# A graph kernel in which SyncE fetches one chunk of 128 edge rows in 64 with one-row DMAs, in place of GpSimd's indirect gather

## The reference

```python
def _gcn_conv(x, src, dst, W, b, n):
    deg = segment_sum(ones_like(dst), dst, n)
    dinv = rsqrt(maximum(deg, 1.0))
    out = segment_sum((x @ W)[src] * (dinv[src] * dinv[dst])[:, None], dst, n)
    return out + b

def _gat_conv(x, src, dst, W, a_src, a_dst, b, n):
    h = (x @ W).reshape(n, H, HID)                    # H = 4, HID = 64
    e = (einsum(h, a_src))[src] + (einsum(h, a_dst))[dst]
    e = where(e > 0, e, 0.2 * e)
    w = exp(e - segment_max(e, dst, n)[dst])
    att = w / segment_sum(w, dst, n)[dst]
    return segment_sum(att[:, :, None] * h[src], dst, n).reshape(n, H * HID) + b

h = batch_norm(relu(_gcn_conv(layernorm(x), ...)))
h = elu(batch_norm(_gat_conv(h, ...)))
h = elu(batch_norm(_gat_conv(h, ...)))
x = x + h
x = x + experts(layernorm(x))                         # 8 experts, top 2
```

## Time and profile before

| | us |
|---|---|
| median of 3 runs | 8761.01 (8760.34 to 8766.04) |
| the profiled execution | 8765.76 |
| its span in the trace | 8763.9 |
| GCN edge stage (391 to 2476 in the span) | 2085 |
| GAT edge stages (2646 to 4735, 5113 to 7202) | 2089 each |
| POOL busy | 5700.4, 65% |
| DVE busy | 4991.6, 57% |
| PE busy | 4960.7, 57% |
| ACT busy | 1673.4, 19% |

### The profile page before, as it was taken

The page is one execution under the profiler, slowest core; times in us unless marked ns, Lnnn a source line. Parts: engine busy times, 40 slices in busy tenths (PEclk is TensorE's granted clock), DMA queues, the critical chain, the costliest instruction groups (busy, mean ns, idle before and its releaser), DMA issues. The chain is left out here.

```text
span 8763.9 us, 120133 instructions
## 1 busy us (share of the span) xinstructions
PE 4960.7 (57%) x24975; PEld 3898.8 (44%) x24976; DVE 4991.6 (57%) x11850; ACT 1673.4 (19%) x7117; POOL 5700.4 (65%) x5675
## 2 busy tenths in 40 slices
PE   3433333333354666666665656666666663369994
PEld 2333333333333444444444434444444442349994
DVE  7722222222237777777777777777777777953335
ACT  3400000000031111111111421111111112253331
POOL 0177777777747777777777467777777776605552
PEclk9999999999997777777777877777777786559997
DMA  5411111111124555555553135555555540212226
GB/s 191 147 26 26 26 26 26 26 26 26 26 68 108 133 133 132 133 133 133 132 133 95 35 99 132 132 133 133 133 133 132 133 127 28 76 63 70 70 70 208
DMA packets 488664, 834.96 MB, mean 95 GB/s; under 512 B 119275, under 2 KB 332904, under 8 KB 481958
## 3 DMA queue, kind: packets, MB, share of 16 engines
q0 software_dynamic: 232576, 551.37, 24.7%
q1 hardware_dynamic: 242740, 270.23, 10.4%
q10 hardware_dynamic: 13298, 12.80, 0.4%
HBM read 751.87 MB, written 82.11 MB: 95 GB/s over the span
## 5 line engine op out<-in xcount | busy, mean ns | idle before, releaser
L707 POOL DMA_INDIRECT gat_rows<-gat_table,gat_idx x3328 | 3202.9, 962 | 1040.1 <-issue 902.4
L771 PE MATMUL gat_ps_sum<-gat_msg,gat_hot 128*128 128x260 f32 x6656 | 2395.4, 522 | 1113.4 <-DVE feat L790 1109.1
L771 PEld LDWEIGHTS gat_ps_sum<-gat_msg,gat_hot 128*128 128x128 f32 x6656 | 1641.9, 259 | 1487.5 <-DVE gat_msg L824 1132.6
L707 POOL DMA_INDIRECT gcn_rows<-gcn_table,gcn_idx x1664 | 1570.3, 944 | 857.8 <-issue 506.2
L771 PE MATMUL gcn_ps_sum<-gcn_rows,gcn_hot 128*128 128x64 f32 x3328 | 809.2, 425 | 1294.4 <-issue 946.6
L771 PEld LDWEIGHTS gcn_ps_sum<-gcn_rows,gcn_hot 128*128 128x128 f32 x3328 | 740.6, 327 | 1363.1 <-issue 1363.1
L790 DVE SCALAR_TENSOR_TENSOR feat<-gcn_ps_sum,in_first,feat 128x64 f32 x416 | 118.1, 284 | 1637.5 <-PE gcn_ps_sum L771 1637.5
L814 DVE TENSOR_TENSOR gat_logit<-gat_rows,gat_near 128x16 f32<-128x16 f32 x832 | 148.8, 179 | 1134.9 <-DMA gat_rows<-gat_table,gat_idx 1129.7
L756 PEld LDWEIGHTS gat_ps_near<-gat_tab,gat_hot_t 128*128 128x128 bf16 x6656 | 265.1, 102 | 898.9 <-issue 724.5
L756 PE MATMUL gat_ps_near<-gat_tab,gat_hot_t 128*128 128x24 bf16 x6656 | 312.1, 178 | 538.5 <-DVE gat_hot L802 534.7
L802 DVE TENSOR_TENSOR gat_hot<-gat_count,mod_t 128x512 f32<-128x512 f32 x832 | 566.5, 681 | 0.1
(11 more groups left out here) (331 smaller groups left out, 7358.4 us busy)
## 6 DMA issues: line engine op xcount, KB each, us to landing
gat_mod<-mod_rows SPq DMA_DIRECT2D x832, 128.0 KB
gi_mods<-mod_rows SPq DMA_DIRECT2D x52, 1024.0 KB, 4.6
gat_rows<-gat_table,gat_idx POOLq DMA_INDIRECT x3328
gcn_rows<-gcn_table,gcn_idx POOLq DMA_INDIRECT x1664, 2.4
gat_table<-feat SPq DMA_DIRECT2D x14, 1820.0 KB, 7.1
mix_rows<-y_rows SPq DMA_DIRECT2D x98, 256.0 KB, 5.1
xn_rows<-ffi_z SPq DMA_DIRECT2D x7, 1792.0 KB, 6.7
out_dram<-feat ACTq DMA_DIRECT2D x48, 256.0 KB
```

The costliest lines, as they stand in the source:

```text
L707: pool.indirect_dma_start(B["rows"][:, c, k, :], None, table, bass.IndirectOffsetOnAxis(ap=B["idx"][:, c, k:k + 1], axis=0)).then_inc(rows ...
L771: mm = pe.matmul(B["ps_sum"][b][:, 0:width], B["hot"][:, j, k, :], rhs, start=(k == 0), stop=(k == CH - 1))
```

## The change

In every edge stage, of each 16 groups the one with number 7 (AT) gets only three indirect DMAs from POOL. The rows of its fourth chunk come another way, all of it issued by SP (`send`, which takes the place of `send_mods` and now runs in the GCN stage too):

1. `bring`, 32 groups ahead: a DMA loads the chunk's 128 source numbers to `ahead_idx`, one partition.
2. `fetch`, 16 groups ahead: in each of 16 turns SP loads eight of the numbers to registers and issues eight DMAs of one row each, from the table to one partition of `ahead` (two buffers).
3. `push`, in turn 6 of the 16: SP waits until all 128 rows are there and until group 16n+3 has been used, and copies `ahead` to the slot of group 16n+7 with one DMA (semaphore `pushed`).
4. `free`, once in 16 turns: waits for the copy before last and for the source numbers.

ACT, PE (GCN) and DVE (GAT) wait for `pushed` in addition where they deal with that group. The loop bodies hold 16 turns instead of 4, SP's 32. The counts by which engines wait for rows are worked out by `landed`, since one slot in four gets 16 increments fewer in each 16 groups.

```diff
+AHEAD, AT = 16, 7
+BURST = P // AHEAD
@@ def edge_buffers
+    B.update(ahead=T.sb("ahead", [P, 2, width]), ahead_idx=T.sb("ahead_idx", [1, 2, P], I32))
@@ def fast_edges
     def gather(pool):
         def group(i, c):
-            g = RING * i + c
+            j, g = c % RING, AHEAD * i + c
             pool.wait_ge(idx_staged, g + 1)
             wait(pool, rows_used, g - 3)
             pool.sem_inc(begun, 1)
-            for k in range(CH):
-                pool.indirect_dma_start(B["rows"][:, c, k, :], None, table,
...
+            for k in range(CH - (c == AT)):
+                pool.indirect_dma_start(B["rows"][:, j, k, :], None, table,
...
-        pace(pool, NG, [(group, 0)], RING)
-
-    def send_mods(sp):
-        def group(i, c):
-            g = RING * i + c
-            wait(sp, hot_built, g - 3)
-            sp.dma_start(B["mod"][:, c, :], mod_rows[one(g), :].to_broadcast([P, GE])).then_inc(mod_in[c], 16)
-        pace(sp, NG, [(group, 0)], RING)
+        pace(pool, NG, [(group, 0)], AHEAD)
+
+    def send(sp):
+        regs = [sp.alloc_register(f"{L}sp_row{r}") for r in range(BURST)]
+        own = AT % RING
+
+        def mods(i, c):
+            j, g = c % RING, 2 * AHEAD * i + c
+            wait(sp, hot_built, g - 3)
+            sp.dma_start(B["mod"][:, j, :], mod_rows[one(g), :].to_broadcast([P, GE])
+                         ).then_inc(mod_in[j], 16)
+
+        def bring(i, c):
+            n, b = 2 * i + c // AHEAD, c // AHEAD % 2
+            if c % AHEAD == 0:
+                at = (AHEAD * n + AT) * GE + (CH - 1) * P
+                sp.dma_start(B["ahead_idx"][0:1, b, :], src[bass.ds(at, P)].rearrange("(a e) -> a e", a=1)
+                             ).then_inc(idx_in[b], 16)
+
+        def free(i, c):
+            n, b = 2 * i + c // AHEAD, c // AHEAD % 2
+            if c % AHEAD == 0:
+                wait(sp, pushed, 16 * (n - 1))
+                sp.sem_inc(ahead_free, 1)
+                sp.wait_ge(idx_in[b], 16 * (i + c // AHEAD // 2 + 1))
+                sp.sem_inc(ahead_free, 1)
+
+        def fetch(i, c):
+            b, part = c // AHEAD % 2, c % AHEAD
+            sp.load(regs, B["ahead_idx"][0:1, b, part * BURST:(part + 1) * BURST])
+            for r in range(BURST):
+                p = part * BURST + r
+                row = sp.snap(regs[r], min_val=0, max_val=S.N - 1)
+                sp.dma_start(B["ahead"][p:p + 1, b, :], table[bass.ds(row, 1), :]).then_inc(ahead_in[b], 16)
+
+        def push(i, c):
+            n, b = 2 * i + c // AHEAD, c // AHEAD % 2
+            if c % AHEAD == AT - 1:
+                sp.wait_ge(ahead_in[b], 16 * P * (i + c // AHEAD // 2 + 1))
+                sp.sem_inc(ahead_free, 1)
+                wait(sp, rows_used, AHEAD * n + (AT - 3))
+                sp.dma_start(B["rows"][:, own, CH - 1, :], B["ahead"][:, b, :]).then_inc(pushed, 16)
+        pace(sp, NG, ([(mods, 0)] if gat else []) + [(free, AHEAD), (bring, 2 * AHEAD), (fetch, AHEAD), (push, 0)], 2 * AHEAD)
@@ def pe_program, total (the same on ACT and in DVE's logits)
-                pe.wait_ge(rows_in[j], 64 * (i + c // RING + 1))
+                pe.wait_ge(rows_in[j], landed(i, c))
+                if c % AHEAD == AT:
+                    pe.wait_ge(pushed, 16 * (i + c // AHEAD + 1))
@@ def build_edges
-            if gat:
-                @block.sync
-                def _(sp):
-                    either(sp, fast["send_mods"], None)
+            @block.sync
+            def _(sp):
+                either(sp, fast["send"], None)
```

More of the change, by code:

```diff
@@ L684, in weights, with fast_edges @@
     return B["weight"][b][:, 0:CH * HEADS].rearrange("p (c h) -> p c h", c=CH)
-def fast_edges(L, M, K, S, B, table, mod_rows, width, gat):
+def fast_edges(L, M, K, S, B, src, table, mod_rows, width, gat):
     NG = S.NG
@@ L698, in fast_edges, with landed @@
     rows_used = msg_made if gat else summed
+    pushed, ahead_free = M.sem(L + "pushed"), M.sem(L + "ahead_free")
+    def landed(i, c):
+        turn, rest = CH * AHEAD // RING, CH * (c // RING + 1)
+        if c % RING == AT % RING:
+            turn, rest = turn - 1, rest - (c // AHEAD + (c % AHEAD >= AT))
+        return 16 * turn * i + 16 * rest
+    idx_in = [M.sem(f"{L}ahead_idx_in{b}") for b in range(2)]
+    ahead_in = [M.sem(f"{L}ahead_in{b}") for b in range(2)]
     def gather(pool):
         def group(i, c):
-            g = RING * i + c
+            j, g = c % RING, AHEAD * i + c
             pool.wait_ge(idx_staged, g + 1)
@@ L722, in stage @@
         def stage(i, c):
-            j, g = c % RING, RING * i + c
-            wait(act, rows_in[j], 64 * (i + c // RING))
+            j, g = c % RING, AHEAD * i + c
+            used = c - RING
+            wait(act, rows_in[j], landed(i, used))
+            if used % AHEAD == AT:
+                wait(act, pushed, 16 * (i + used // AHEAD + 1))
             act.copy(B["idx"][:, j, :], at1(K["src_t"], g)).then_inc(idx_staged, 1)
@@ L738, in weigh @@
         def weigh(i, c):
-            g = RING * i + c
+            g = AHEAD * i + c
             act.wait_ge(logit_step, 4 * g + 4)
@@ L743, in weigh @@
             act.activation(B["msg"][:, c % 2, :, FEAT:ROW], B["logit"][:, c % 2, :, :], ACT.Exp).then_inc(weighed, 1)
-        pace(act, NG, [(weigh, 2), (stage, RING + 2)] if gat else [(stage, RING)], RING)
+        pace(act, NG, [(weigh, 2), (stage, RING + 2)] if gat else [(stage, RING)], AHEAD)
     def pe_program(pe):
         def look(i, c):
-            j, g, b = c % RING, RING * i + c, c % 2
+            j, g, b = c % RING, AHEAD * i + c, c % 2
             pe.wait_ge(hot_built, g + 1)
@@ L773, in total @@
             mm.then_inc(summed, 1)
-        pace(pe, NG, [(total, 1), (look, 3)] if gat else [(total, 0)], RING)
+        pace(pe, NG, [(total, 1), (look, 3)] if gat else [(total, 0)], AHEAD)
     def dve_program(dve):
@@ L780, in add @@
         def add(i, c):
-            g, b = RING * i + c, c % 2
+            g, b = AHEAD * i + c, c % 2
             if c % RING == 0:
@@ L812, in logits @@
                                    AX, ALU.add))
-            dve.wait_ge(rows_in[j], 64 * (i + c // RING + 1))
+            dve.wait_ge(rows_in[j], landed(i, c))
+            if c % AHEAD == AT:
+                dve.wait_ge(pushed, 16 * (i + c // AHEAD + 1))
             link(dve.tensor_tensor(logit, B["rows"][:, j, :, FEAT:ROW], near[:, :, 0:HEADS], ALU.add))
@@ L826, in dve_program @@
         steps = [(messages, 1), (add, -1), (logits, 2), (hots, 3)] if gat else [(add, 0), (hots, 3)]
-        pace(dve, NG, steps, RING)
-    return dict(gather=gather, send_mods=send_mods, act=act_program, pe=pe_program, dve=dve_program)
+        pace(dve, NG, steps, AHEAD)
+    return dict(gather=gather, send=send, act=act_program, pe=pe_program, dve=dve_program)
 def general_buffers(T, gat):
@@ L969, in any_edges, with build_edges @@
     return dict(gather=gather, act=act_program, pe=pe_program, dve=dve_program)
-def build_edges(nc, L, M, K, S, table, mod_rows, width, gat, flag):
+def build_edges(nc, L, M, K, S, src, table, mod_rows, width, gat, flag):
     with ExitStack() as scope:
@@ L979, in build_edges @@
             B["weight"] = [G["ps_rel"], G["ps_as"]]
-        fast = fast_edges(L, M, K, S, B, table, mod_rows, width, gat)
+        fast = fast_edges(L, M, K, S, B, src, table, mod_rows, width, gat)
         slow = any_edges(L, M, K, S, B, G, table, width, gat)
@@ L1433, in build_gnn @@
             flag = build_attention(nc, L, T, K, S, table)
-            build_edges(nc, L, T, K, S, table, mod_rows, ROW, True, flag)
+            build_edges(nc, L, T, K, S, src, table, mod_rows, ROW, True, flag)
             build_batch_norm(nc, L, T, K, S, FEAT, bias, gamma, beta, gat=True)
```

8 lines of the change are left out of this document (4 added, 4 removed).

## The result

The changed kernel takes **8814.22 us** (8813.91 to 8815.55, 4 runs) where the kernel before takes 8763.53 (8760.34 to 8766.07) beside it: ratio **1.0058**, interval [1.0045, 1.0072]. It is 50.7 us slower. The profiled execution took 8814.23 us with a span of 8812.5, against 8765.76 and 8763.9. The number lies in the range of 8700 to 9130, but outside the 17.5 us that were to count as "no change", and outside the forecast's own 8742 to 8785.

A forecast was written before the change was run, and what follows sets the result against it. POOL's issue of gathers, one every 1.25 us, was taken as the bound. GCN +12.0 and both GAT stages -5.8 gave +6 us: 8772 on the profiled execution, 8767 on the median, no change; range 8700 to 9130.

The forecast's parts named there:

- The gain: POOL, each edge stage: 26 gathers fewer at 1.25 us, 32.5 us saved; 31.2 in GCN, one gather swallowed by a wait.
- Rival 4: Gather landings set the group pace, or longer loops stall engines beyond the ring's cover; gain gone, 8863 us, chance 0.05.
- The row DMA: On SP: each one-row DMA (its cost called D) takes 255 ns, so a row costs 0.45 us and eight 3.6.
- Rival 2: On SP: the row DMA is much cheaper than any row shows; 8696 us at D = 0.10, floor 8664, chance 0.20.
- rival 3: One DMA engine carries all rows and falls behind, so copies come late: 83 us a stage, 9020 us, chance 0.07.
- The register load: On SP, each turn: a TENSOR_LOAD of registers takes 0.34 us, and a gap.
- SP's turn in GAT: SP needs 4.66 us a group, POOL leaves 4.92: SP is not the bound, with 5% to spare.
- rival 1: SP becomes the bound of the GAT stages, from D = 0.28 on; 9124 us at 0.333; chance 0.30 in all.
- The longer loops "at no cost": Bodies unrolled 16 and 32 times cost nothing: fewer loop branches, covered by the ring's 10.7 us.
- The starts: Stage starts, SP's 128 row DMAs ahead of first mods and copy: POOL loses 43.2 us in GCN, 29.6 per GAT stage.
- The sum: Whole kernel: 12.0 for GCN less 5.8 for both GAT stages, +6 us; 8767 on the median, no change.
- SP should still wait at the copy in the later half of a GAT stage: Expected sign in SP's trace: SP ahead of need, 74.6 us between copies against POOL's 78.7.

The follow-up runs named there:

- E10: Changed kernel, but POOL alone gathers each stage's first 16 groups and SP loads 16 registers every second turn: 8670.35 us, ratio 0.9895 to the kernel before.
- E4: Changed kernel, but SP loads 16 registers every second turn instead of 8 every turn: 8789.41 us, ratio 1.0016 to the kernel before.
- E6: Changed kernel with SP's loop unrolled 64 times instead of 32: 8786.00 us, ratio 1.0028 to the kernel before.
- E1: Changed kernel's longer loops alone: POOL gathers all four chunks, SP sends only the mods: 8776.45 us, ratio 1.0002 to the kernel before.
- E3: Changed kernel, but POOL alone gathers the first 16 groups of each stage: 8686.06 us, ratio 0.9900 to the kernel before.
- E9: Repeat of the changed kernel with POOL alone gathering each stage's first 16 groups: 8681.15 us, ratio 0.9909 to the kernel before.
- E2: Changed kernel, but SP copies its rows to an unread spare buffer and POOL gathers all chunks: 8845.38 us, ratio 1.0080 to the kernel before.

## Why the prediction was right and wrong

- **The gain** of 32.5 us a stage, counted as 31.2 in GCN with one gather inside the wait: right. Rival 4 falls with the gathers' even 1.25 us. By the Trainium skill ("DMA: Bandwidth & Descriptors", Issuing engines are not separate DMA queues) the issue time that is saved is usually small; for this kernel the runs disagree, for E10 gets 92.6 us out of issue time alone.
- **The row DMA**, taken as 255 ns: 218 in GCN and 228 in GAT, so a row is 0.41 to 0.42 us and not 0.45. The row of 103 partitions was a near guess, 27 to 37 ns too high. Rival 2 would have needed about 100, and nothing near 600 or 881 came up. The rows are not spread over the DMA engines (from 2670 to 2700, 57 of them make 112 packets on SP's queue, two each) and still don't fall behind (rival 3): before the copies SP waited once for landings, 1.1 us in GCN.
- **The register load**, 0.34 us, is the term that was mis-sized. I took the price of four registers on DVE for eight on SP, and the earlier trace rows can't be scaled without a second size. Eight cost 0.72 to 0.78. It adds 0.38 to 0.44 a turn, and the cheaper rows give 0.3 (GCN) and 0.2 (GAT) back. In GCN the plain turn is 4.11 in place of 3.98. By the Trainium skill ("DMA: Bandwidth & Descriptors", Latency and other measured facts) such a load has a floor of about 600 ns. Four registers on DVE at 344 ns lie under that, but for eight it would have been a better guess than mine.
- **SP's turn in GAT**, 4.66 us against POOL's 4.92 and so "5% to spare": this is the step that failed. A plain turn alone is 4.68. I had put the loop branch, waits and the rest at 0.15 a group "from the same rows", but no row before shows SP at a loop end without idle time around it. They cost 3.75 / 32 = 0.12 for the loop end, 0.36 / 4.5 = 0.08 for the fetches within, and about 0.1 for the turns with the copy and the index load: 4.98, where 4.965 and 4.99 were measured. In the prediction's own terms: 4.66, + 0.38 for the load, - 0.22 for the rows, + 0.15 for the rare parts, which are 0.30 and not 0.15, make 4.97. So rival 1 came true at its very edge, though by another cause than the one I priced: the point at which it decides lay at D = 0.28, D was 0.228, and what closed the gap was the load and the instruction fetch. E4 and E6 show both: each of them alone takes nearly all the breaks away.
- **The longer loops "at no cost"**: I counted their branches and not what one costs, 2.9 to 4.0 us on SP and 2.2 to 3.0 on DVE. DVE's lie far under the 10.7 us of cover and cost nothing where SP is on time (E1, E10). With SP late that cover is used up, and it is at them that the breaks show. What the breaks would be without DVE's stops is open; SP's mean turn says about the same.
- **The starts**: in GCN 43.2 predicted, which is 44.4 of idle time with the saved gather in it, and 48.2 of idle time measured; 29.6 and 34.3 to 34.4 in GAT. (The terms for GCN add up to 489.7, not the 489.9 written; nothing hangs on it.) The mechanism was right to the group of POOL at which it shows. In GAT the mods went out after 69.4 us, not 66.4, by the loads; mods(1) came 5.06 us later, not 4.5; it took 2.9 us to DVE, not 2.3; and the gather starts 0.8 us behind the end of the messages, for which I had nothing.
- **The sum**: +6 predicted, +48 measured. Of the 42 between them the starts are 3.7 + 4.7 + 4.8 = 13.2 and the breaks some 29. The forecast put 0.31 on "within 0.2%" and 0.43 on "slower"; the likeliest single case was the wrong one. That the time lies in the range is luck as far as the forecast goes: its own 8742 to 8785 missed, and the range was that wide only for a row DMA of 333 ns, which did not come.
- **"SP should still wait at the copy in the later half of a GAT stage"**: wrong for the most part. It waited for the group before the copy 12 times in 52, 23.0 us in all, of which one is 9.7; between 5400 and 7100 these waits are 3.1 us.

## What to carry to other kernels

- Offloading a bit of a bounding engine's work to an idle one pays by the difference of two turns. Write out the idle engine's whole turn, with its rare parts spread over it (loop end, instruction fetch, the wide turn), for 5% of room is less than what these add up to.
- Work that is fetched ahead comes due in one block at the start, where nothing covers it. Let the old way serve the first round: here that alone turned a loss of 51 us into a gain of 82 to 88 (E3, E9).
- A loss that comes at the period of a loop's length points at that loop's end; halve the ends or shorten the turn and look whether it goes. Look at the other engines' loop ends too: here SP's turn set how much was lost, and DVE's loop end where it showed.

## What the runs showed of the hardware that I had not expected

- A loop end of SP with a long body (32 turns of some thirty instructions) stops it for 2.9 to 4.0 us, in which the trace has one or two packets of the instruction queue; doubling the body leaves it at 3 us. On the page of the whole program that queue grows from 32 packets to 606, of which the longer loops alone, without SP's rows, make 277 (E1).
- DVE stops 2.2 to 3.0 us at each end of a loop of 16 turns, and not once in the kernel before with loops of four (44 times against none). While it has room nobody sees it in the time (E1: 106.2 us of stops, ratio 1.0002).
- A load of registers on SP is 272 ns and 56 for each register (from the two sizes, 8 and 16); straight code of SP stalls 0.36 us about every fourth or fifth turn, beside a fetch packet.
- DMAs of one row issue in 218 ns for 256 bytes and 228 for 1040, on SP, and 9984 of them did not slow the gathers beside them (E2).
